# The first stage of an 8-expert layer rewritten: transposed input, rows scattered whole to their slots, expert blocks loaded by plain transfers

## The chip, the cores and the metric

The kernel runs on one core of a Trainium2 chip. The metric is the device time of one execution in microseconds. A core has the engines PE (matmul), DVE (elementwise, reductions), ACT (activations, copies), POOL (here: the indirect DMAs) and SP (plain DMAs). They run on their own and wait for each other by semaphores.

## The reference

x is 128 x 64 x 256 (8,192 tokens of 256 values). A modulated linear layer makes `hidden`; a top-2 router sends each token to 2 of 8 experts of at most CAP = 2,560 tokens; each expert is a two-layer network 256 → 1,024 → 256 with GELU; the weighted outputs are added to x.

```python
ys  = cond_1024 / sqrt(256)
d   = rsqrt((ys * ys) @ (w * w) + 1e-8)
hid = ((x * ys[:, None, :]) @ w) * d[:, None, :]        # per batch of 64 tokens
logits = hid @ wr.T                                      # 8192 x 8
vals, idx = top_k(logits, 2);  gate = softmax over the two
pos = cumsum(mask) - 1;  keep = pos < 2560               # slot of a token in its expert
h = gelu(hid[tokens of e] @ w1[e] + b1[e])
y = (h @ w2[e] + b2[e]) * gate
out = x + sum of y over a token's experts
```

## The kernel before

**Stage 1** goes over 16 groups of 512 tokens (4 tiles of 128). For each group PE transposes x (L436), DVE multiplies it by ys out of PSUM (L684, `scale_x`), PE multiplies by w (L473, four matmuls 128x512 in fp32, eight records), DVE multiplies by d (L741, `scale_hidden`). From that, with features on partitions, PE makes the logits (L485, 16 records) and transposes the rows back (L493); ACT copies the rows (L616) and stores them to `hidden` in DRAM (L619). DVE copies the logits (L803) and finds first and second expert, mask, gates (L811 to L853: a chain of small operations on 128x32, each of which waits for the one before). PE turns the mask into positions (L458 to L465, bf16), DVE turns these into addresses in a table in DRAM (`begin_list`, `slots`, `pay`), and POOL writes 128 entries of 8 bytes (token, gate) with each indirect DMA (L317): 8 a group, 128 in all. In DVE's order the end of the list of group g−1 stands behind the copy of the logits of group g. SP loads x (L275), stores it to out (L270), and reloads the buffer once that is written.

**Expert stage.** The tokens of an expert lie in blocks of 384 slots (SUBS = 3 tiles), at least LEAST (4) an expert and at most 7. The number is computed on the chip (`plan`). POOL gathers the rows of a block from `hidden` by the ids of the table (L324, three DMAs; L332 and L333 copy the ids), three blocks ahead. PE transposes them (L514), ACT and DVE split them into a high and a low part (L632, L903), and for each of 8 chunks f PE does a first product (L524 to L526, six matmuls 128x384), ACT the GELU (L645, twice), DVE the low part (L909), PE a second product (L536 to L538, nine matmuls 128x256) three chunks later. At a block's end DVE adds the bias (L934), multiplies by the gate (L940), and POOL adds the rows to out with three accumulating indirect DMAs (L357), of which L371 copied the ids. ACT copies an expert's bias once (L663). Weights (2 MB an expert) are loaded by SP and split by ACT and DVE during the two first blocks of the expert before. The last block also transposes and opens a block that does not exist.

The orders on the queues that the change touches: POOL runs scatters, then per block begin of adds, gathers, end of adds; SP runs x and out per group, then weights; PE runs in each block first product 2, transposes of the next block, first product 3, and so on.

Of the kernel before, what the change touches and what calls it, by code (L numbers as in the profile page):

```python
# [15 lines left out]
P = 128  # L25
# [7 lines left out]

TILES = 4
ROWS = TILES * P
GROUPS = T // ROWS
GB = ROWS // S
SUBS = 3
SLOTS = SUBS * P
BLOCKS = -(-CAP // SLOTS)  # L40
LEAST = 4
LAG = 3
TILES_E = BLOCKS * SUBS
COLS = E * TILES_E + SUBS
TABLE = P * COLS
# [3 lines left out]
assert ROWS == 512 and T % (4 * ROWS) == 0  # L49
# [5 lines left out]
NO_SLOT = float(1 << 22)  # L55
BIG = 3.0e38


def build(nc, x, cond, w, wr_t, w1, b1_t, w2, b2, ident, tri, expert_low, slot_base, token_ids,
          plan_consts, empty_table, out):  # L60
    hidden = nc.dram_tensor("hidden", [T + PAD, D], F32, kind="Internal").ap()
    table = nc.dram_tensor("table", [TABLE, 2], I32, kind="Internal").ap()


    x_rows = x.rearrange("b s d -> (b s) d").rearrange("(g j p) d -> g p j d", j=TILES, p=P)
    out_rows = out[0:T, :].rearrange("(g j p) d -> g p j d", j=TILES, p=P)
    hidden_rows = hidden[0:T, :].rearrange("(g j p) d -> g p j d", j=TILES, p=P)
    table_rows = table.rearrange("(p c) v -> p c v", p=P)
# [3 lines left out]
    with ExitStack() as ctx:  # L72
# [9 lines left out]
        ident_sb = sb("ident", [P, P])  # L82
# [6 lines left out]
        cond_sb = sb("cond", [P, D])  # L89
        w_sb = sb("w", [P, KC, D])  # L90
        wsq_sb = sb("wsq", [P, KC, D])
        wr_sb = sb("wr", [P, KC, E])
# [4 lines left out]
        zero_sb = sb("zero", [P, D])  # L97
        plan_sb = sb("plan_consts", [P, BLOCKS + (E + 1) * E])
        steps_e = sb("steps_e", [P, E, BLOCKS])
# [3 lines left out]
        plan_f = sb("plan_f", [P, E + 1])  # L103
        plan = sb("plan", [P, 2 * (E + 1)], I32)
# [8 lines left out]

        x_sb = [sb(f"x{u}", [P, TILES, D]) for u in range(2)]
        xs_t = sb("xs_t", [P, KC, ROWS])
        hid_t = sb("hid_t", [P, KC, ROWS])
        hid_sb = [sb(f"hid{u}", [P, TILES, D]) for u in range(2)]
        RE = [P, TILES, E]
        logits = sb("logits", RE)
# [5 lines left out]
        of_group = sb("of_group", [P, E], BF16)  # L125
# [3 lines left out]
        top = sb("top", [P, 2, TILES])  # L129
        low = sb("low", [P, 2, TILES])  # L130
        gap = sb("gap", [P, TILES])
        ratio = sb("ratio", [P, TILES])
        total = sb("total", [P, TILES])
        picked = sb("picked", [P, 2, TILES, E])
        slot_of = sb("slot_of", [P, 2, TILES], I32)
        low_bits = sb("low_bits", [P, 2, TILES], I32)
        high_bits = sb("high_bits", [P, 2, TILES], I32)
        slots = [sb(f"slots{u}", [P, 2, TILES], I32) for u in range(2)]
        pay = [sb(f"pay{u}", [P, 2, TILES, 2], I32) for u in range(2)]

# [4 lines left out]
        table_sb = sb("table", [P, COLS, 2], I32)  # L145
        table_first = sb("table_first", [P, LAG * SUBS, 2], I32)
        filled = sb("filled", [P, 1], I32)
        gather_ids = sb("gather_ids", [P, SUBS], I32)
        add_ids = sb("add_ids", [P, SUBS], I32)
        ids_ring = sb("ids_ring", [P, 4 * SUBS], I32)  # L150
        xg_first = sb("xg_first", [P, SUBS, D])
        xg_third = sb("xg_third", [P, SUBS, D])
        xg = sb("xg", [P, SUBS, D])
# [6 lines left out]
        y_sb = [sb(f"y{s}", [P, D]) for s in range(SUBS)]  # L160


        first_in = sem("first_in")
        const_in = sem("const_in")
        late_in = sem("late_in")
        table_empty = sem("table_empty")
        pad_zero = sem("pad_zero")
        set_dve = sem("set_dve")
        set_pe = sem("set_pe")
# [3 lines left out]
        x_loaded = [sem(f"x_loaded{u}") for u in range(2)]  # L173
        hid_stored = [sem(f"hid_stored{u}") for u in range(2)]
        scattered = [sem(f"scattered{u}") for u in range(2)]
        out_written = sem("out_written")
        added = sem("added")
        y_free = sem("y_free")
        t_done = sem("t_done")
# [3 lines left out]
        l_done = sem("l_done")  # L183
        back_done = sem("back_done")
        hid_copied = sem("hid_copied")
        step = sem("step")
        counted = sem("counted")
        mask_ready = sem("mask_ready")
        pos_done = sem("pos_done")
        gap_ready = sem("gap_ready")  # L190
        ratio_ready = sem("ratio_ready")
        pay_ready = sem("pay_ready")
# [3 lines left out]
        totals_done = sem("totals_done")  # L196
        plan_step = sem("plan_step")
        plan_ready = sem("plan_ready")

        first_loaded = sem("first_loaded")  # L200
        filled_ready = sem("filled_ready")
        table_loaded = sem("table_loaded")
        gather_listed = sem("gather_listed")
        add_listed = sem("add_listed")
        gathered_first = sem("gathered_first")
        gathered_third = sem("gathered_third")
        gathered = sem("gathered")
# [16 lines left out]
        h_bank = [bank[4], bank[5], bank[7]]  # L224
        out_filled = 16 * (SUBS + GROUPS)

        PEEL = 4

        FILLING = GROUPS - 3

# [767 lines left out]
```

## Time and profile before

| | |
|---|---|
| median of 3 runs | 1087.09 us (1080.96 to 1089.59) |
| profiled execution, its own time | 1081.37 us |
| its span | 1079.6 us |
| mean granted PE clock | 0.938 |
| PE busy | 978.0 us (91%) |
| DVE busy | 498.2 us (46%) |
| ACT busy | 487.9 us (45%) |
| POOL busy | 542.5 us (50%), 550 instructions |

Durations in a profile come from one execution. A line of the timeline or of a group names line, engine and operation, out<-in with the program's names, and the shape. In brackets stands the idle time before it and what ended it; "remote" and "another core or an unknown queue" mean that the profile found no instruction whose end fits the release. PEclk is the granted clock as a part of full speed.

### The profile page before, as it was taken

Reading aid. Unit: us, or ns where it says so; the run is one execution under the profiler, and the core shown is the slowest. Engines: PE = TensorE matmul, PEld = TensorE weight load, DVE = VectorE, ACT = ScalarE, POOL = GpSimd, SP = SyncE. Lnnn points to the kernel's source line nnn. Section 1 sums busy time; section 2 is a strip of 40 time slices with the busy share of each in tenths; the row PEclk is TensorE's granted clock in tenths of the full one; section 3 lists DMA queues with packets and bytes.
Section 4 is the critical chain, followed back from the end, with each engine's and each line's share of the span. In section 5 each row is a group of like instructions: output and inputs, shape, how many; then the busy total and the mean of one; then the engine's idle time right before and its main releaser. Section 6 shows DMA issues by size and latency. Waiting matters only on the chain.

```text
span 1079.6 us, 20555 instructions
## 1 busy us (share of the span) xinstructions
PE 978.0 (91%) x6550; PEld 925.8 (86%) x6551; DVE 498.2 (46%) x1395; ACT 487.9 (45%) x968; POOL 542.5 (50%) x550
## 2 busy tenths in 40 slices
PE   7588787439999999999999999999999999999994
PEld 4365555239999999999999999999999999999994
DVE  5454455254444534453455445444444453445342
ACT  3000001015556555655565555556555555565552
POOL 0545665753545454545454554545454536454542
PEclk9877778659999999999999999999999999999997
DMA  8454332321433432343224322432422242222322
GB/s 287 143 152 140 118 117 59 99 87 58 127 42 53 110 58 35 53 111 54 39 49 112 53 45 42 117 49 44 121 49 39 49 116 49 39 49 39 53 35 29
DMA packets 71071, 84.18 MB, mean 78 GB/s; under 512 B 11008, under 2 KB 64000, under 8 KB 70912
## 3 DMA queue, kind: packets, MB, share of 16 engines
q0 software_dynamic: 30880, 37.12, 20.8%
q1 hardware_dynamic: 30352, 37.86, 10.7%
q10 hardware_dynamic: 9824, 9.03, 2.6%
q8 instruction: 6, 0.10, 0.0%
q14 instruction: 9, 0.07, 0.0%
HBM read 47.80 MB, written 35.96 MB: 78 GB/s over the span
## 4 chain that ended last, share of the span: by engine, by line
PE 78%; another core or an unknown queue 7%; DVE 7%; issue 3%; DMA 2%; POOL 1%; ACT 0%; DVEq 0%; POOLq 0%; SPq 0%; ACTq 0%
PE bank L526 12%; PE bank L524 12%; PE bank L525 11%; PE bank L536 11%; PE bank L537 11%; PE bank L538 11%; PE bank L514 3%; PE bank L473 2%; PE bank L436 2%; PE bank L485 2%; DMA out_rows<-sb_y,sb_add_ids 1%; PE bank L493 1%; DVE sb_xs_t L684 1%; POOL out_rows L357 1%
## 5 line engine op out<-in xcount | busy, mean ns | idle before, releaser
L645 ACT ACTIVATE sb_h_raw<-bank,sb_b_now 128x384 f32<-128x384 f32 x370 | 216.4, 585 | 313.7 <-PE bank L526 297.1
L909 DVE TENSOR_TENSOR sb_h_lo<-sb_h_raw,sb_h_hi 128x384 fp32r<-128x384 f32 x370 | 206.1, 558 | 328.8 <-ACT sb_h_hi L645 298.9
L536 PE MATMUL bank<-sb_w_hi,sb_h_hi 128*128 128x256 f32 x1104 | 310.1, 281 | 0.8 <-DVE sb_y L934 0.8
L537 PE MATMUL bank<-sb_w_lo,sb_h_hi 128*128 128x256 f32 x1104 | 309.5, 280 | 0.0
L538 PE MATMUL bank<-sb_w_hi,sb_h_lo 128*128 128x256 f32 x1104 | 308.1, 279 | 0.0
L524 PE MATMUL bank<-sb_xt_hi,sb_w_hi 128*128 128x384 f32 x740 | 258.2, 349 | 12.4 <-DVE sb_xt_lo L903 11.7
L357 POOL DMA_INDIRECT out_rows<-sb_y,sb_add_ids x138 | 229.4, 1662 | 66.7 <-POOL sb_add_ids L371 34.9
L525 PE MATMUL bank<-sb_xt_lo,sb_w_hi 128*128 128x384 f32 x740 | 251.0, 339 | 0.8 <-issue 0.8
L526 PE MATMUL bank<-sb_xt_hi,sb_w_lo 128*128 128x384 f32 x740 | 250.5, 339 | 0.4 <-issue 0.4
L645 ACT ACTIVATE sb_h_hi<-bank,sb_b_now 128x384 fp32r<-128x384 f32 x370 | 213.1, 576 | 0.0
L536 PEld LDWEIGHTS bank<-sb_w_hi,sb_h_hi 128*128 128x128 f32 x1104 | 207.4, 188 | 1.4 <-DVE sb_y L934 1.4
L538 PEld LDWEIGHTS bank<-sb_w_hi,sb_h_lo 128*128 128x128 f32 x1104 | 207.9, 188 | 0.0
L537 PEld LDWEIGHTS bank<-sb_w_lo,sb_h_hi 128*128 128x128 f32 x1104 | 207.5, 188 | 0.0
L317 POOL DMA_INDIRECT table<-sb_pay,sb_slots x128 | 125.6, 981 | 112.8 <-DVE sb_slots L762 69.1
L324 POOL DMA_INDIRECT sb_xg<-hidden,sb_gather_ids x132 | 137.1, 1038 | 66.7 <-POOL sb_ids_ring L333 38.3
L371 POOL COPY sb_add_ids<-sb_ids_ring 128x3 int32 x46 | 15.9, 345 | 280.8 <-DVE sb_y L940 280.8
L524 PEld LDWEIGHTS bank<-sb_xt_hi,sb_w_hi 128*128 128x128 f32 x740 | 139.7, 189 | 16.5 <-issue 16.4
L525 PEld LDWEIGHTS bank<-sb_xt_lo,sb_w_hi 128*128 128x128 f32 x740 | 140.3, 190 | 0.4 <-issue 0.4
L526 PEld LDWEIGHTS bank<-sb_xt_hi,sb_w_lo 128*128 128x128 f32 x740 | 139.8, 189 | 0.5 <-issue 0.5
L616 ACT COPY sb_hid<-bank 128x512 f32<-128x512 f32 x32 | 17.2, 588 | 176.7 <-remote 146.1
L485 PE MATMUL bank<-sb_wr,sb_hid_t 128*128 128x8 f32 x256 | 43.3, 306 | 38.2 <-DVE sb_hid_t L741 38.2
L485 PEld LDWEIGHTS bank<-sb_wr,sb_hid_t 128*128 128x128 f32 x256 | 42.6, 260 | 40.6 <-DVE sb_hid_t L741 39.7
(110 smaller groups left out, 789.6 us busy)
## 6 DMA issues: line engine op xcount, KB each, us to landing
sb_w_raw<-in_w SPq DMA_DIRECT2D x18, 1024.0 KB
out_rows<-sb_x SPq DMA_DIRECT2D x16, 512.0 KB
hidden<-sb_hid ACTq DMA_DIRECT2D x16, 512.0 KB
sb_x<-in_x SPq DMA_DIRECT2D x15, 512.0 KB
out_rows<-sb_y,sb_add_ids POOLq DMA_INDIRECT x138
sb_xg<-hidden,sb_gather_ids POOLq DMA_INDIRECT x132
table<-sb_pay,sb_slots POOLq DMA_INDIRECT x128
sb_b<-in_b SPq DMA_DIRECT2D x1, 1024.0 KB, 9.0
```

What stands on the lines that cost most here:

```text
L317: pool.indirect_dma_start(table, bass.IndirectOffsetOnAxis(slots[u][:, c, j:j + 1], axis=0), pay[u][:, c, j, :], None, bounds_check=TABLE ...
L324: pool.indirect_dma_start(into[:, s, :], None, hidden, bass.IndirectOffsetOnAxis(block_ids[:, s:s + 1], axis=0),).then_inc(landed, 16)
L357: pool.indirect_dma_start(out, bass.IndirectOffsetOnAxis(add_ids[:, s:s + 1], axis=0), y_sb[s][:, :], None, compute_op=ALU.add,).then_inc( ...
L485: mm = pe.matmul(bank[6][:, j * E:(j + 1) * E], hid_t[:, k, j * P:(j + 1) * P], wr_sb[:, k, :], start=(k == 0), stop=(k == KC - 1))
L524: pe.matmul(h, w_hi[u][:, cols], xt_hi[:, rows], start=(k == 0), stop=False)
L525: pe.matmul(h, w_hi[u][:, cols], xt_lo[:, rows], start=False, stop=False)
L526: mm = pe.matmul(h, w_lo[u][:, cols], xt_hi[:, rows], start=False, stop=(k == KC - 1))
L536: pe.matmul(y, hi, w_hi[u][:, cols], start=(f == 0), stop=False)
L537: pe.matmul(y, hi, w_lo[u][:, cols], start=False, stop=False)
L538: mm = pe.matmul(y, lo, w_hi[u][:, cols], start=False, stop=(f == FC - 1))
L645: ins = act.activation(h[f % RING][:, :], h_bank[f % H_BANKS][:, 0:SLOTS], ACT.Gelu_apprx_tanh, bias=b1_now[u][:, f:f + 1])
L909: dve.tensor_tensor(h_lo[f % RING][:, :], h_raw[f % RING][:, :], h_hi[f % RING][:, :].bitcast(F32), ALU.subtract).then_inc(h_ready, 1)
```

## The change

- x is also given transposed (`x_t`, 256 x 8,192), cond too. SP loads columns of a group into a ring of four buffers; `scale_x` multiplies them in place. Transposes L436 are gone.
- Rows and logits come from one pair of matmuls for each tile of 128 tokens (`turn_back`): the moving operand is 136 columns, the identity and half of wr beside it; both halves' logits add up in the eight columns between the two blocks of 128. The result goes into one of three PSUM banks and ACT copies it (128x264) into a row of 272 floats: 128 values, 8 logits (later gates), 128 values, token id. A ring of 5 such sets in SBUF takes the place of `hid` and of `hidden` in DRAM.
- Routing works on sets of two groups (TS = 8 tiles, 8 sets): `choose` in each even group, `positions` on PE, `find_slots` and `list_set` on DVE in each odd one, from group 3 on. The gates of all eight experts are written into the row.
- POOL scatters whole rows of 1,088 bytes into `slot_rows` in DRAM, by expert and slot: 16 DMAs a set, 128 in all. It waits for the set's list and for the landing of the set two before.
- A block is then one plain load of SP (`load_block`, 384 rows, 418 KB). It waits for the transposes of the block before (`t_done`) and for DVE's copies of gates and ids (`take_meta`, `meta_done`). Blocks 0 to 3 of expert 0 are loaded as soon as the sets that fill them are placed (`need`), block 4 after all sets are placed and the unfilled slots are filled (`fill_holes`, about one transfer of 418 KB an expert).
- In a block PE's transposes of the next block move from behind first product 2 to between first product 6 and second product 3.
- POOL keeps only the adds; gathers, id copies and the table are gone. The outputs of blocks 0 to 3 have buffers of their own, since POOL adds them after the last scatter.
- out gets x by copies from DRAM to DRAM (`copy_x`), 8 in stage 1, 8 beside the early blocks.
- The last block opens no other. LEAST is 5 instead of 4.

```diff
+            def scale_x(g):
+                tile = x_in[g % X_RING]
+                dve.wait_ge(x_loaded[g % X_RING], 16 * (g // X_RING + 1))
+                for k in range(KC):
+                    cols = tile[:, k, :].rearrange("p (b s) -> p b s", s=S)
+                    dve.tensor_tensor(cols, cols, by_batch(ys_t, k, g), ALU.mult).then_inc(xs_ready, 1)
...
+            for g in range(GROUPS):
+                s = g // 2 - 1
                 scale_hidden(g)
+                if g + 2 < GROUPS:
+                    scale_x(g + 2)
+                if g % 2 == 0 and g >= 2:
+                    choose(s)
+                if g % 2 == 1 and g >= 3:
+                    found = find_slots(s)
+                    if s == SETS - 2:
+                        early_needs()
+                    list_set(s, found)
+                if 3 <= g < 3 + PIECES:
+                    split_piece(0, g - 3, g - 2)
```

PE:

```diff
+            def turn_back(g):
 
                 pe.wait_ge(hid_ready, KC * (g + 1))
                 for j in range(TILES):
+                    t = g * TILES + j
+                    tile = back_bank[t % 3]
+                    if t >= 3:
+                        pe.wait_ge(row_copied, t - 2)
+                    pe.matmul(tile[:, 0:P + E], hid_t[g % 2][:, 0, j * P:(j + 1) * P], back_sb[:, 0:P + E],
+                              start=True, stop=True)
+                    pe.matmul(tile[:, P:2 * P + E], hid_t[g % 2][:, 1, j * P:(j + 1) * P],
+                              back_sb[:, P + E:2 * (P + E)], start=False, stop=True,
+                              skip_group_check=True).then_inc(back_done, 1)
...
+            modulate(0)
+            for g in range(1, GROUPS):
+                modulate(g)
+                if g >= 3 and g % 2 == 1:
+                    positions((g - 3) // 2)
+                turn_back(g - 1)
+            turn_back(GROUPS - 1)
...
                 first_product(u, 2)
-                pe.wait_ge(gathered, b * (16 * SUBS) + 16 * SUBS)
-                transpose_block()
...
+                for f in range(3, FC):
                     bank_read(b, f - 3)
                     first_product(u, f)
+                    if f == 3:
+                        pe.wait_ge(y_read, b * SUBS + SUBS)
+                    if f - 3 == TURN and u_next is not None:
+                        pe.wait_ge(block_loaded, b * 16 + 32)
+                        transpose_block()
                     chunk_split(b, f - 3)
                     second_product(u, f - 3)
```

POOL and SP:

```diff
+            for s in range(SETS):
+                if s >= 2:
+                    pool.wait_ge(placed[s % 2], sets_placed(s - 2))
+                else:
+                    pool.wait_ge(slots_zero, 16)
+                pool.wait_ge(list_ready, s + 1)
+                for j in range(TS):
                     for c in range(TOP_K):
                         pool.indirect_dma_start(
+                            slot_rows, bass.IndirectOffsetOnAxis(slots[s % ROW_RING][:, c, j:j + 1], axis=0),
+                            rows[s % ROW_RING][:, j, :], None, bounds_check=SLOT_ROWS - 1, oob_is_err=False,
+                        ).then_inc(placed[s % 2], 16)
...
+            def load_block(e, j, b):
+                sp.wait_ge(t_done, b)
+                sp.sem_inc(sp_paced)
+                sp.wait_ge(meta_done, b)
+                sp.sem_inc(sp_paced)
+                sp.dma_start(xg[:, :, :], block_rows(e, j)).then_inc(block_loaded, 16)
```

## Rows read from the trace of the kernel before

**Rows 1.** Windows of the whole run; engines' busy time (instructions), PEclk, DMA share, GB/s.

```profile
160.00:180.00 20.00, 16.01 (x74) 10.29 (x73) 11.56 (x59) 2.56 (x6) 11.56 (x12) 0.83 0.26 79
...
400.00:640.00 240.00, 238.94 (x1709) 237.70 (x1709) 111.23 (x237) 132.82 (x262) 120.43 (x121) 1.00 0.32 61
```

**Rows 2.** Timeline; start us, us, engine, line, operation: first first-product; bias copies.

```profile
239.31 0.66 PE L524 MATMUL bank<-sb_xt_hi,sb_w_hi 128*128 128x384 f32 x1 [6.71 <-DVE sb_xt_lo L903]
...
330.95 0.22 ACT L663 COPY sb_b_now<-sb_b 128x8 f32 x1
...
954.40 0.21 ACT L663 COPY sb_b_now<-sb_b 128x8 f32 x1
```

**Rows 3.** Page, part 5: count | busy us, mean ns | idle before.

```profile
L357 POOL DMA_INDIRECT out_rows<-sb_y,sb_add_ids x138 | 229.4, 1662 | 66.7 <-POOL sb_add_ids L371 34.9
...
L317 POOL DMA_INDIRECT table<-sb_pay,sb_slots x128 | 125.6, 981 | 112.8 <-DVE sb_slots L762 69.1
L324 POOL DMA_INDIRECT sb_xg<-hidden,sb_gather_ids x132 | 137.1, 1038 | 66.7 <-POOL sb_ids_ring L333 38.3
```

**Rows 4.** Page, part 4: what the chain that ended last consists of.

```profile
PE 78%; another core or an unknown queue 7%; DVE 7%; issue 3%; DMA 2%; POOL 1%; ACT 0%; DVEq 0%; POOLq 0%; SPq 0%; ACTq 0%
```

**Rows 5.** Timeline of one group, stage 1; in brackets idle before and releaser.

```profile
162.47 0.19 DVE L836 TENSOR_TENSOR sb_first<-sb_expert_low,sb_low 128x32 f32<-128x32 f32 x1
...
163.17 0.97 POOL L317 DMA_INDIRECT table<-sb_pay,sb_slots  x1 [2.07 <-issue]
...
166.06 2.91 PE L485 MATMUL bank<-sb_wr,sb_hid_t 128*128 128x8 f32 x16 [0.49 <-DVE sb_hid_t L741]
...
172.12 0.97 POOL L317 DMA_INDIRECT table<-sb_pay,sb_slots  x1 [0.31 <-issue]
...
174.69 0.19 DVE L803 COPY sb_logits<-bank 128x32 f32<-128x32 f32 x1 [5.89 <-remote]
...
176.59 0.97 POOL L317 DMA_INDIRECT table<-sb_pay,sb_slots  x1 [3.50 <-DVE sb_slots L762]
```

**Rows 6.** Timeline of the first stream of scatters.

```profile
33.31 1.86 PE L485 MATMUL bank<-sb_wr,sb_hid_t 128*128 128x8 f32 x16
...
35.93 3.60 PE L473 MATMUL bank<-sb_xs_t,sb_w 128*128 128x512 f32 x8
...
50.02 0.97 POOL L317 DMA_INDIRECT table<-sb_pay,sb_slots  x1 [0.30 <-issue]
...
53.59 1.29 DVE L741 TENSOR_TENSOR sb_hid_t<-bank,sb_d_t 128x512 f32<-128x512 f32 x2 [12.01 <-remote]
```

**Rows 7.** Waits of 60 to 200 us: total us, times, longest.

```profile
ACT sb_hid L616 <- remote: 106.9, 10, 11.1
DVE sb_logits L803 <- remote: 52.0, 11, 6.0
```

**Rows 8.** Timeline beside six weight pieces.

```profile
234.54 3.69 DVE L720 TENSOR_TENSOR sb_w_lo<-sb_w_raw,sb_w_hi 128x512 fp32r<-128x512 f32 x6
...
236.38 1.50 POOL L317 DMA_INDIRECT table<-sb_pay,sb_slots  x1 [0.31 <-issue]
```

**Rows 9.** Chain of waits: start us, us, what.

```profile
15.93 1.21 DVE sb_hid_t L741 x2
```

**Rows 10.** DMA issues: count, KB each, us from issue to landing.

```profile
sb_b<-in_b SPq DMA_DIRECT2D x1, 1024.0 KB, 9.0
...
sb_table<-table SPq DMA_DIRECT2D x1, 171.0 KB, 2.6
```

**Rows 11.** Timeline of the end.

```profile
1065.08 0.28 PE L538 MATMUL bank<-sb_w_hi,sb_h_lo 128*128 128x256 f32 x1
...
1066.27 0.34 DVE L940 TENSOR_SCALAR sb_y<-sb_y,sb_table 128x256 f32<-128x256 f32 x1
...
1067.30 0.35 DVE L940 TENSOR_SCALAR sb_y<-sb_y,sb_table 128x256 f32<-128x256 f32 x1 [0.18 <-issue]
1067.96 1.58 POOL L357 DMA_INDIRECT out_rows<-sb_y,sb_add_ids  x1 [0.80 <-DVE sb_y L940]
```

More of the change, by code:

```diff
@@ new lines, in _ @@
+            n_holes = sp.value_load(holes[0:1, E:E + 1], min_val=E, max_val=E * LEAST)
+            sp.wait_ge(filled, n_holes * 16 + 16)
+            sp.sem_inc(sp_paced)
+            for s in range(SETS - 2, SETS):
+                sp.wait_ge(placed[s % 2], sets_placed(s))
+            sp.wait_ge(plan_ready, 1)
+            _, end = plan_of(sp, 0)
+            with sp.Fori(EARLY, end) as b:
+                load_block(0, b, b)
+            sp.wait_ge(w_lo_done, PIECES * 2)
+            load_weights(2)
@@ L424, in _ @@
-            rest = all_blocks(pool, less=1)
-            one_block(rest, E * TILES_E)
-            for i in (1, 2):
-                begin_adds(rest + i)
-                end_adds(rest + i)
+                    pool.indirect_dma_start(
+                        out, bass.IndirectOffsetOnAxis(ids[:, s:s + 1], axis=0),
+                        y[s], None, compute_op=ALU.add,
+                    ).then_inc(added, 16)
+                pool.wait_ge(added, b * (16 * SUBS) + 16 * SUBS)
+            for j in range(EARLY):
+                add_block(y_early[j], add_early[j], j)
@@ L732, in over_e, with whole, mark, after @@
                 return a.unsqueeze(2).to_broadcast(RE)
-            SPLIT_GROUPS = (0, GROUPS - 1)
+            def whole(make, *args):
+                with nc.allow_low_precision(reason="whole numbers below 2**24"):
+                    return make(*args)
+            count = [0]
+            def mark(ins):
+                count[0] += 1
+                ins.then_inc(step, 1)
+                return count[0]
+            def after(n):
+                dve.wait_ge(step, n)
             def scale_hidden(g):
+                if g >= 2:
+                    dve.wait_ge(back_done, TILES * (g - 1))
@@ new lines, in expert @@
+            def expert(u, e, start, end):
+                for j in range(2):
+                    one_block(u, e, start + j, j * len(SPLIT_AT), y_later, add_later)
+                with dve.Fori(start + 2, end) as b:
+                    one_block(u, e, b, None, y_later, add_later)
+            _, end = plan_of(dve, 0)
+            for j in range(EARLY):
+                one_block(0, 0, j, j * len(SPLIT_AT) if j < 2 else None, y_early[j], add_early[j], early=True)
+            with dve.Fori(EARLY, end) as b:
+                one_block(0, 0, b, None, y_later, add_later)
@@ L954, in constants @@
+            with dve.Fori(0, E // 2 - 1) as pair:
+                for u in (1, 0):
+                    e = pair * 2 + (2 - u)
+                    start, end = plan_of(dve, e)
+                    expert(u, e, start, end)
+            start, end = plan_of(dve, E - 1)
+            with dve.Fori(start, end - 1) as b:
+                one_block(1, E - 1, b, None, y_later, add_later)
+            one_block(1, E - 1, end - 1, None, y_later, add_later, last=True)
 def constants():
     p = np.arange(P)
-    empty = np.zeros((TABLE, 2), np.int32)
```

948 lines of the change are left out of this document (433 added, 515 removed).

## The prediction

> **What bounds the kernel now.** I read the table of windows first [rows 1]. From 400 us on PE is busy all but one microsecond in 240 at clock 1.00: the expert stage is bound by PE. Ahead of it, from 0 to the first first-product at 239.31 [rows 2], PE is busy by half to four fifths at a granted clock of 0.83 in the window shown. So the span is a first stage of 239 us that nothing fills and 46 blocks that PE fills: the adds number 138, three to a block [rows 3].
>
> The price of a block comes from the bias copies, one at the start of each expert [rows 2]. Eight of them stand in the trace; the gaps between are 96, 107, 107, 106, 90, 107 and 108 us, so experts have 5, 6, 6, 6, 5, 6, 6 blocks and the last has 6. Between the second and the last, 35 blocks take 954.40 − 330.95 = 623.45 us, 17.81 us each.
>
> The chain of waits [rows 4] then gives 7% of the span to "another core or an unknown queue". The timeline of one group [rows 5] shows what that is. The 16 router matmuls L485 end at 166.06 + 2.91 = 168.97, yet the copy of their result, L803, starts at 174.69 after 5.89 us idle; POOL issues the eight scatters of a group from 163.17 to 173.09. PE's completion is seen only once the stream of scatters is over. In a stream of 16 it is worse: PE's L473 end near 35.93 + 3.60 = 39.5, DVE's L741 that needs them starts at 53.59, 2.6 us after the stream's end at 50.99 [rows 6]. The waits of 60 to 200 us sum it: ACT 106.9 us in 10 waits and DVE 52.0 us in 11, all of them for PE results [rows 7]. So in the first stage POOL's scatters set the pace twice: 128 of them, and each burst holds the next group back. Of a group's 13.4 us (163.17 to 176.59) the burst is 9.9.
>
> **The change, part by part.** 46 blocks (LEAST 5 adds none, as every expert has at least 5) stay as they are, but for the last, which loses the next block's transposes (six records, 0.7 us) and two idle first products (2 × 1.06): −2.8 us.
>
> *PE and DVE in stage 1.* Transposes of x go; rows and logits come from 16 matmul records of 136 columns a group in place of 16 + 8 records. The records of 128x512 take 3.60 us a group at full clock [rows 6]; 16 records of 136 columns lie between L485's pace of 0.116 (1.86 for 16 [rows 6]) and that of 512 columns: I take 2.0 us, and 0.3 for the positions. So PE needs 5.9 us a group. DVE for two groups has 4 pairs of 128x512 at 1.29 [rows 6], 13 dependent routing steps like L836 (0.19 [rows 5], here on twice the elements; with the step between them I take 0.25: 3.2), the list, some ten such steps, 2.5, and two weight pieces at 3.69 / 6 [rows 8] 1.3: 12.2 us, 6.1 a group. ACT's four copies of 128x264 move what its two of 128x512 did, and are hidden. Both engines end at about 6.1 a group. The first L741 was at 15.93 [rows 9]; its successor stays near 16.5. Stage 1 for PE would end at 16.5 + 16 × 6.1 + 5 = 119, if no one holds it.
>
> *POOL.* The same count, 128 scatters, but of 1,088-byte rows instead of 8 bytes. Issue is 0.98 us and a gap of 0.30 for 8 bytes [rows 3, 6], 1.04 for a gather of 1 KB rows, 1.66 for an accumulating scatter of 1 KB rows [rows 3]. So the price of one lies between 1.28 and 1.96 us. A plain write is nearest to the gather (no read of the target): 1.04 + 0.30 = 1.34. To this comes DVE: under six L720 (both inputs in SBUF) a scatter took 1.50 in place of 0.97 [rows 8], 0.53 us for 3.69 us of such work. scale_x now has both inputs in SBUF (before, one was PSUM): 2.6 us of it for 16 scatters, 0.03 each. 1.37 × 128 = 175.4 us. The first list is ready at 16.5 + 3 × 6.1 + 2 = 36.8. Last scatter issued 212.2, landed 2.5 later (the hold's release came 2.6 after a stream [rows 6]): 214.7.
> The Trainium skill ("SBUF — State Buffer", SBUF: two separate sides) says that a DVE operation with two SBUF inputs holds a lock against GpSimd operations which read SBUF, and blocks them whole. The stretched scatter agrees in direction, at 0.53 us for six such operations and not for each; were each in-place multiply to block for its whole 0.65 us, 32 × 0.65 = 21 us would come in place of the 4 counted, and the sum would be 1008 instead of 991.
>
> *The start of the blocks.* By my count of the routing of these inputs (token sets of 1,024) expert 0's blocks 0 to 3 need 2, 4, 6 and 7 sets, so they run at 119 to 204 with small stalls: set 7 is placed at 192, block 3's load wants 184. Block 4 needs all eight. Its load: 418 KB between a load of 171 KB at 2.6 us and one of 1,024 KB at 9.0 [rows 10], by the line between them 4.4, with 0.4 to issue. So block 4's transposes start at 214.7 + 4.8 = 219.5, inside block 3, of which 9.3 us are then left (transposes 0.7, five second products, three first products). From there 42 blocks × 17.81 = 748.0.
>
> *Gathers, ids, the table* (132 gathers and 4 copies a block) leave POOL, which then has only the adds: three by 1.96, 5.9 us of 17.8. In the steady state the next block's load is issued when DVE has multiplied the old block (2.3 us after its last matmul: 1067.65 against 1065.36 [rows 11]) and copied gates and ids, in all some 3.5 us into the block; it lands 4.4 later at 7.9, and its transposes stand at 17.8 − 9.3 = 8.5: hidden by 0.6 us, and what it is later than that comes on every block. Copying x to out without passing SBUF moves the same bytes; the DMA share is 0.26 in the group's window [rows 1], no limit. One fill of 418 KB per expert lies under blocks.
>
> *Tail.* Before, 1079.6 − 1065.36 (end of the last matmul [rows 11]) = 14.2 us; the ids copy between the first multiply's end (1066.61) and the first add (1067.96) goes, 1.3 us: 12.9.
>
> *Sum.* 219.5 + 9.3 + 748.0 − 2.8 + 12.9 = 986.9 us of span. The profiled execution of before took 1081.37 for a span of 1079.6: +1.8, 988.7. Its median was 5.7 above that, its lowest 0.4 below; I add the middle, 2.5: **991 us**.
>
> Bounds of this case: 1.28 a scatter, −11.5; every in-place multiply costing the 0.53 us seen once, 32 × 0.53 − 4 = +13; landing times and the stalls before block 4, −9 to +16: 970 to 1020. At 1.96 a scatter, +75: 1066.
>
> **Rivals.**
> *The hold repeats* (the other side). Scatters now come 16 at a time, 21.9 us, and nearly without pause, while PE's ring of three row banks and every list hang on PE completions. For it: 21 such waits in 140 us [rows 7], and the longest behind the longest stream [rows 6]. Against it: in the block stage POOL is as busy (120 of 240 us [rows 1]) with gathers and adds of 1 KB rows beside a PE that hardly stops, so long rows or short streams may be spared. If it repeats whole, a set takes the stream 21.9, release 1.7, and then what waited: rest of the turn-back 2.6, choose 3.2, positions 0.6, list 2.2, a pause q of 10.3. PE then starts the blocks at 36.8 + 7 × (21.9 + q) + 3 = 193 + 7q = 265 and nothing later stops it: 46 × 17.81 + 2.1 − 2.8 = 818.6, + 12.9 + 1.8 and 2.5: 1101. In general 1029 + 7q: no gain from q = 8.3 on, slower than 1% from q = 10.
> *A partial hold*: DVE's mean wait now is 52.0 / 11 = 4.7 us [rows 7]; with q between 0 and 6 the time is 1030 to 1071, where the accumulate's price for a scatter falls too.
> *PE sets the pace* (scatters overlap better than their records show, or issue is shorter for long rows): 119 + 818.6 + 4.8 for plan and list + 12.9 + 1.8 = 957.
> *Block loads come late.* Load, gates and ids are one chain through DVE; each microsecond late costs some 45. From 2.1 us late on (a load of 7.1 us in place of 4.4) the gain of 96 us is gone. On SP an expert's last block load stands ahead of 2 MB of weights, and the next block load behind their issue; two transfers of 1,024 KB at 9.0 [rows 10] are over before it in all but the shortest wait. Against late loads: 1 MB took those 9.0 us beside other loads.
>
> **How the numbers follow.** POOL-paced, 970 to 1020: 0.44; forecast 991. PE-paced, about 957: 0.05. Partial hold or dear scatters, 1030 to 1071: 0.19. Full hold, 1075 to 1110: 0.27. Late loads, above 1050: 0.05. About 1% is what a measurement of this kernel can tell from no change, so the bounds are 1076 and 1098: faster 0.44 + 0.05 + 0.19 + 0.01 = 0.69; the hold is shared between same, 0.14, and slower, 0.17. The range for 8 in 10 leaves out the PE-paced case and the upper part of the hold: 965 to 1102; the likeliest case alone has 970 to 1020.
>
> **What would show it.** Right: first first-product near 119; scatters back to back at 1.34 to 1.40 from 37 to 212; no idle longer than 2 us before the row copies on ACT; block 4's transposes right behind the last scatter. The hold: row copies and L741's successor idle "remote" until a stream's end, gaps of 5 to 10 us between streams, first product after 200. Late loads: PE idle at each block before the transposes, released by the block load. Wrong price: scatter records above 1.3 us. The sum is wrong if the block's pace moves from 17.8, because 46 multiplies it.

## The result, and the profile after

| | before | after |
|---|---|---|
| median | 1086.26 us (4 runs, 1080.96 to 1089.59) | 1052.47 us (4 runs, 1046.39 to 1057.75) |
| ratio after / before | | 0.969, 95% interval 0.9625 to 0.9758 |
| profiled execution, span | 1079.6 us | 1049.7 us |
| first first-product | 239.31 | 208.77 |

The kernel is 3.1% faster. The forecast was 991 us, 95 less than before; 34 came. The time lies in the range given, and in the place of the rival "a partial hold" (1030 to 1071). Medians and ratios, here and below, are of fast runs: runs more than 1.5% above the fastest of the same kernel in their group are left out.

The windows of the changed kernel's run, as in [rows 1] (engines' busy time with counts in the order PE, PE's weight loads, DVE, ACT, POOL, then PEclk, DMA share, GB/s):

```profile
60.00:80.00 20.00, 6.93 (x12) 3.28 (x12) 0.31 (x1) 0.76 (x2) 15.14 (x16) 0.59 0.44 162
...
100.00:120.00 20.00, 17.52 (x94) 10.58 (x92) 16.11 (x57) 5.59 (x15) 15.66 (x14) 1.00 0.87 266
...
140.00:160.00 20.00, 0.60 (x3) 0.28 (x2) 3.71 (x13) 0.00 (x0) 14.52 (x15) 0.50 0.28 100
...
400.00:640.00 240.00, 240.00 (x1733) 239.32 (x1732) 114.26 (x276) 133.32 (x265) 63.80 (x40) 1.00 0.34 72
```

The expert stage is filled as before: PE is busy 240.00 of 240. But of the first stage, PE is busy 6.93 us in one window of 20 and 0.60 in another, while POOL is busy 15.14 and 14.52 in the same two. In the window from 100 on, with POOL just as busy, PE gets 17.52. The timeline of the worst stretch (start us, us, engine, line; in brackets the idle time before and its releaser):

```profile
142.02 0.97 POOL L363 DMA_INDIRECT slot_rows<-sb_rows,sb_slots  x1 [1.52 <-DVE sb_rows L793]
...
147.46 0.69 DVE L734 TENSOR_TENSOR sb_hid_t<-bank,sb_d_t 128x512 f32<-128x512 f32 x1 [6.30 <-remote]
...
157.91 0.69 DVE L734 TENSOR_TENSOR sb_hid_t<-bank,sb_d_t 128x512 f32<-128x512 f32 x1 [9.77 <-remote]
...
161.63 0.97 POOL L363 DMA_INDIRECT slot_rows<-sb_rows,sb_slots  x1 [0.30 <-issue]
164.91 0.38 ACT L583 COPY sb_rows<-bank 128x264 f32<-128x264 f32 x1 [25.53 <-remote]
...
165.34 0.82 PE L417 MATMUL bank<-sb_back,sb_hid_t 128*128 128x136 f32 x2 [24.74 <-ACT sb_rows L583]
...
166.40 6.00 PE L405 MATMUL bank<-sb_x,sb_w 128*128 128x512 f32 x8
...
174.44 3.60 PE L405 MATMUL bank<-sb_x,sb_w 128*128 128x512 f32 x8
...
177.84 0.97 POOL L363 DMA_INDIRECT slot_rows<-sb_rows,sb_slots  x1 [15.24 <-DVE sb_rows L793]
```

POOL issues the 16 scatters of a set without a gap from 142.02 to 162.60. In that time DVE's L734 is let through twice, after 6.30 and 9.77 us of idle, for matmuls that had ended long before; ACT's row copy L583 waits 25.53 us and starts 2.3 us after the last scatter is issued, and PE then starts at once (165.34), because its ring of row banks waited for that copy. The trace also records when a semaphore was updated: the matmuls that this copy waited for ended at 140.60, and their update is recorded at 164.88. POOL in turn stands idle for 15.24 us until the list of the next set, 177.84. This is the picture of [rows 5] and [rows 6], with longer streams.

A hold costs twice, since PE comes out of it at the lower clock: the windows above show a granted clock of 0.59 and 0.50 (the 1.2 GHz level) where PE is busy for 6.93 and 0.60 us of 20, and 1.00 (2.4 GHz) where it is busy for 17.52. The eight records of 128x512 from 166.40 take 6.00 us, those from 174.44 take 3.60.

The waits of 0 to 260 us (total us, times, longest):

```profile
ACT sb_rows L583 <- remote: 73.3, 11, 25.5
...
DVE sb_hid_t L734 <- remote: 18.3, 3, 9.8
```

The blocks start, and the stall in block 0 that is again a result seen late:

```profile
208.77 0.65 PE L472 MATMUL bank<-sb_xt_hi,sb_w_hi 128*128 128x384 f32 x1 [0.34 <-issue]
...
227.32 0.55 PE L484 MATMUL bank<-sb_w_hi,sb_h_hi 128*128 128x256 f32 x1 [4.82 <-remote]
```

The bias copies, one an expert, of which these are the first, the second and the last (as in [rows 2]):

```profile
208.40 0.18 ACT L626 COPY sb_b_now<-sb_b 128x8 f32<-128x8 f32 x1
...
319.79 0.21 ACT L626 COPY sb_b_now<-sb_b 128x8 f32 x1
...
931.48 0.21 ACT L626 COPY sb_b_now<-sb_b 128x8 f32<-128x8 f32 x1
```

From 319.79 to 931.48 are 35 blocks: 17.48 us each, against 17.81. Expert 0 has 111.39 us for its 5 blocks, 24.0 more than 5 × 17.48. The window over them shows where they went:

```profile
208.80:320.00 111.20, 94.64 (x613) 92.39 (x614) 45.24 (x125) 49.47 (x99) 48.39 (x41) 0.89 0.56 156
```

PE is idle for 16.6 us of it and busy for 94.64 where five blocks at full clock need 87.4: some 7 of the 24 us come with the granted clock of 0.89. The page's groups (count | busy us, mean ns | idle before), as in [rows 3]:

```profile
L375 POOL DMA_INDIRECT out_rows<-sb_y,sb_add_later x126 | 201.4, 1598 | 525.3 <-DVE sb_y L915 471.7
...
L472 PE MATMUL bank<-sb_xt_hi,sb_w_hi 128*128 128x384 f32 x736 | 250.8, 341 | 9.3 <-issue 3.6
...
L363 POOL DMA_INDIRECT slot_rows<-sb_rows,sb_slots x128 | 129.4, 1011 | 120.9 <-issue 79.6
```

The scatter of 1,088 bytes takes 1,011 ns a record, 30 more than the one of 8 bytes and 27 less than the gather. The end, as in [rows 11]:

```profile
1037.85 0.28 PE L486 MATMUL bank<-sb_w_hi,sb_h_lo 128*128 128x256 f32 x1
...
1039.81 1.54 POOL L375 DMA_INDIRECT out_rows<-sb_y,sb_add_later  x1 [9.13 <-DVE sb_y L915]
```

The last matmul ends at 1038.13, 11.6 us before the span's end (before: 14.2).

### The profile page after: what moved, and what is told of

Its sections match the earlier page's. It is cut to its first block, busy times and chain, and to the rows that moved or that the text cites. A ratio compares the mean times of both kernels' runs of the same rounds, so it can differ in the third digit from the quotient of the medians.

```text
span 1049.7 us, 18506 instructions
## 1 busy us (share of the span) xinstructions
PE 923.2 (88%) x6284; PEld 877.7 (84%) x6285; DVE 477.8 (46%) x1264; ACT 483.1 (46%) x978; POOL 350.7 (33%) x270
## 3 DMA queue, kind: packets, MB, share of 16 engines
q1 hardware_dynamic: 38496, 58.32, 18.5%
q0 software_dynamic: 26016, 35.93, 18.5%
## 4 chain that ended last, share of the span: by engine, by line
PE 84%; another core or an unknown queue 6%; issue 5%; DVE 2%; ACT 1%; DMA 0%; POOL 0%; POOLq 0%; DVEq 0%; ACTq 0%
PE bank L474 13%; PE bank L472 12%; PE bank L473 12%; PE bank L484 12%; PE bank L485 12%; PE bank L486 12%; PE bank L405 4%; PE bank L462 3%; PE bank L417 2%; PE bank L419 1%; ACT sb_rows L583 1%; DMA sb_ys_t<-in_cond_t 0%; POOL out_rows L375 0%; DVE sb_x L676 0%
## 5 line engine op out<-in xcount | busy, mean ns | idle before, releaser
L375 POOL DMA_INDIRECT out_rows<-sb_y,sb_add_later x126 | 201.4, 1598 | 525.3 <-DVE sb_y L915 471.7
L484 PE MATMUL bank<-sb_w_hi,sb_h_hi 128*128 128x256 f32 x1104 | 313.5, 284 | 5.9 <-remote 4.8
L472 PE MATMUL bank<-sb_xt_hi,sb_w_hi 128*128 128x384 f32 x736 | 250.8, 341 | 9.3 <-issue 3.6
L486 PEld LDWEIGHTS bank<-sb_w_hi,sb_h_lo 128*128 128x128 f32 x1104 | 211.0, 191 | 0.5 <-issue 0.5
L363 POOL DMA_INDIRECT slot_rows<-sb_rows,sb_slots x128 | 129.4, 1011 | 120.9 <-issue 79.6
L583 ACT COPY sb_rows<-bank 128x264 f32<-128x264 f32 x64 | 23.9, 379 | 163.5 <-remote 73.3
L417 PE MATMUL bank<-sb_back,sb_hid_t 128*128 128x136 f32 x128 | 30.9, 327 | 64.2 <-issue 38.3
L823 DVE TENSOR_TENSOR sb_xt_lo<-bank,sb_xt_hi 128x384 fp32r<-128x384 f32 x92 | 47.0, 552 | 78.8 <-ACT sb_xt_hi L601 73.9
L417 PEld LDWEIGHTS bank<-sb_back,sb_hid_t 128*128 128x128 f32 x128 | 22.9, 216 | 70.6 <-issue 43.6
L601 ACT CAST sb_xt_hi<-bank 128x384 fp32r<-128x384 f32 x92 | 39.6, 481 | 83.3 <-PE bank L474 77.4
```

The source lines that it names most:

```text
L363: pool.indirect_dma_start(slot_rows, bass.IndirectOffsetOnAxis(slots[s % ROW_RING][:, c, j:j + 1], axis=0), rows[s % ROW_RING][:, j, :], N ...
L375: pool.indirect_dma_start(out, bass.IndirectOffsetOnAxis(ids[:, s:s + 1], axis=0), y[s], None, compute_op=ALU.add,).then_inc(added, 16)
L417: pe.matmul(tile[:, 0:P + E], hid_t[g % 2][:, 0, j * P:(j + 1) * P], back_sb[:, 0:P + E], start=True, stop=True)
L472: pe.matmul(h, w_hi[u][:, cols], xt_hi[:, rows], start=(k == 0), stop=False)
L484: pe.matmul(y, hi, w_hi[u][:, cols], start=(f == 0), stop=False)
L486: mm = pe.matmul(y, lo, w_hi[u][:, cols], start=False, stop=(f == FC - 1))
```

## The experiments

The theory after these traces: a stream of indirect DMAs issued by POOL keeps PE's completions from being seen (**theory A**). Against it: the first stage is slow by its own chain of PE, DVE and ACT (**B**).

The kernels ran in six groups, each on one chip together with the kernel before. Before took 1021 to 1022 us in three of them (e1, e4, e5; single runs 1020.5 to 1024.2) and 1076 to 1090 in the other three (e2, e3, e6; single runs 1074.2 to 1098.8), near the 1086 of the first result. I call these groups without and with the hold. No trace of the kernel before is from a group without it, so for that kernel the hold's absence there is read from the time alone. One chip number stands on both a group with (e2) and one without (e5), so what decides it is not known. Times are compared within a group. The kernels without the sorting and e3_indirect_seq ran once each.

| kernel | group | before | this | first first-product |
|---|---|---|---|---|
| rows stored by ACT's queue (e1_plain_hw) | without | 1021.3 | 937.0 | 113.7 |
| the same (e4_plain_hw) | without | 1022.0 | 936.6 | 113.3 |
| plain DMAs of POOL (e1_plain_sw) | without | 1021.3 | 933.9 | 114* |
| the same (e2_plain_sw) | with | 1076.1 | 932.4 | 112.6 |
| changed kernel (e5_after) | without | 1022.0 | 975.0 | 119.4 |
| changed kernel (e2_after) | with | 1076.1 | 1040.7 | 199.5 |
| changed kernel (e3_after) | with | 1090.2 | 1044.3 | 199.0 |
| indirect, consecutive addresses (e3_indirect_seq) | with | 1090.2 | 1043.4 | 203* |
| landing awaited every 4 (e1_paced4) | without | 1021.3 | 1056.3 | 151* |
| the same (e3_paced4) | with | 1090.2 | 1055.5 | 149.7 |
| every 8 (e1_paced8) | without | 1021.3 | 1014.9 | 134.0 |
| the same (e3_paced8) | with | 1090.2 | 1017.1 | 132.0 |
| every 16 (e4_paced16) | without | 1022.0 | 993.9 | 125.8 |
| the same (e5_paced16) | without | 1022.0 | 994.5 | 126* |
| the same (e6_paced16) | with | 1086.2 | 1029.0 | 186.2 |
| 4 fills after every 8 (e4_work8) | without | 1022.0 | 1015.1 | 129.8 |
| before, paced (e4_before_paced4) | without | 1022.0 | 1099.7 | 260.4 |

(*: read from the first bias copy or from the first record that the trace kept.)

### Without POOL's indirect DMAs

The edit of the plain DMAs of POOL, in short; in all kernels of this part a fixed fill also takes the place of the holes, and in the form with ACT's queue two DMAs a set take the place of POOL's loop:

```diff
-                        pool.indirect_dma_start(slot_rows, IndirectOffsetOnAxis(slots[...]), rows[...][:, j, :], ...)
+                        first = s * ROWS_E + (c * TS + j) * P
+                        pool.dma_start(slot_rows[first:first + P, :], rows[s % ROW_RING][:, j, :])
```

e1_plain_hw: 

> Left out: the sorting of rows to experts. POOL scatters nothing; ACT's queue stores the 1,024 rows of set s twice, in order, into the slots of expert s (2 plain DMAs a set in place of 16 indirect ones, same bytes), and a fixed fill takes the place of the holes. Theory A (a stream of DMAs issued by POOL keeps PE's completions from being seen): no 'remote' wait of more than 2 us in stage 1, first first-product near 120 instead of 208.8, expert 0 without its 24 us of stalls, span 1049.7 - 89 - 24 = 937. Theory B (the first stage is slow by its own chain PE, DVE, ACT, whatever POOL does): first first-product at 200 or later, span 1040 or more.

e1_plain_sw: 

> Left out: the sorting of rows to experts. POOL issues the same 16 DMAs a set of 128 rows of 1,088 bytes, but plain ones to consecutive rows in place of indirect ones; a fixed fill takes the place of the holes. Theory A (any stream of DMAs whose descriptors POOL makes): remote waits of 10 us and more as in the changed kernel, first first-product within 185 to 225, span 1030 to 1065. Theory C (it is the indirect form or the scattered addresses): like the kernel with plain stores from ACT's queue, first first-product near 120 to 150, span 940 to 990.

e2_plain_sw: 

> Left out: the sorting of rows to experts (plain DMAs of POOL to consecutive rows in place of indirect ones, a fixed fill in place of the holes). On the other chip it took 934 us with no remote wait. If this chip is of the kind where before takes 1086: Theory A (any stream of DMAs of POOL holds PE) 1030 to 1065 with remote waits; Theory C (only indirect ones) 934 again. If this chip is of the kind of 1021: 934 again under both, and the indirect form itself is what costs against it.

e4_plain_hw: 

> Left out: the sorting of rows to experts (2 plain DMAs of ACT's queue a set). The price of everything but the scatters, on this chip: 935 as on the other one, with the first first-product near 114, whichever kind the chip is.

The two rows of e2_plain_sw, POOL's first 16 DMAs and the first first-product, in a group with the hold:

```profile
40.87 8.76 POOL L364 DMA_DIRECT2D slot_rows<-sb_rows  x16 [40.44 <-DVE sb_rows L792]
...
112.61 0.66 PE L471 MATMUL bank<-sb_xt_hi,sb_w_hi 128*128 128x384 f32 x1 [1.10 <-issue]
```

Theory B falls: with the same chain of PE, DVE and ACT the first stage ends at 113 us. No wait of these kernels ends on "remote". The plain form is also cheaper to issue, 8.76 us for 16, 0.55 each. That makes its streams short and puts a pause of 2 to 3 us behind each, so these runs alone don't tell the form from the length.

### The changed kernel in both kinds of group

e2_after: 

> The changed kernel again, as it is. The four runs before were made on a chip on which the kernel before takes 1021 us in place of 1086. Theory A' (PE's completions are held behind POOL's streams, and how much depends on the chip): on a chip where before takes about 1021, no remote waits, first first-product near 120, POOL's 128 scatters end by 41 + 171 = 212, block 4 and all after it follow from there: span 212 + 2 + 4.8 + 9.3 + 42 x 17.48 - 2.8 + 11.6 = 971, gain 5%; on one where it takes about 1086, 1050 again with first first-product near 209, gain 3%. Theory D (that chip is faster in everything, by 6%): after at 1050 x 0.94 = 987 with its first first-product at 196 and the same remote waits.

e2_before: 

> The kernel before again, for its trace on this chip. Theory A': where it takes about 1021 us, the waits of L616 and L803 for remote are gone and the first first-product comes near 239 - 60 = 179, while the pace of a block stays at 17.8 us. Theory D: the pace of a block is 16.8.

e5_after: 

> The changed kernel as it is. On a chip where before takes about 1022 (no hold): 975, first first-product near 120, last scatter near 212. On a chip that holds: 1044 again.

The kernel before, profiled in the group e2 (which turned out to be one with the hold; first first-product at 257.3), with its waits as in [rows 7], here of 0 to 260 us:

```profile
ACT sb_hid L616 <- remote: 146.4, 12, 19.2
...
DVE sb_logits L803 <- remote: 49.5, 11, 5.8
```

The changed kernel in e5, without the hold: first first-product, last scatter, load of block 4, its transposes; then its bias copies, and what is waited for until 300 us.

```profile
119.42 0.66 PE L472 MATMUL bank<-sb_xt_hi,sb_w_hi 128*128 128x384 f32 x1 [0.22 <-issue]
...
212.32 1.11 POOL L363 DMA_INDIRECT slot_rows<-sb_rows,sb_slots  x1 [0.31 <-issue]
...
215.91 0.42 SPq L295 DMA_DIRECT2D sb_xg<-slot_rows  x1
...
220.00 1.54 PE L462 MATMUL bank<-sb_back,sb_xg 128*128 128x128 f32 x6 [7.00 <-DMA sb_xg<-slot_rows]
```

Its second and last bias copy:

```profile
243.93 0.22 ACT L626 COPY sb_b_now<-sb_b 128x8 f32 x1
...
855.67 0.21 ACT L626 COPY sb_b_now<-sb_b 128x8 f32<-128x8 f32 x1
```

```profile
PE bank L462 <- DMA sb_xg<-slot_rows: 29.9, 4, 18.8
...
ACT sb_rows L583 <- DMA slot_rows<-sb_rows,sb_slots: 10.4, 1, 10.4
```

No wait is "remote" now, although POOL issues 113 scatters in a row from 41.47 to 191.47; PE waits for block loads, that is for POOL's scatters, as the forecast had it. Theory D (everything 6% faster) falls: the pace of a block is 17.48 in both e5_after (855.67 − 243.93 = 611.74 us for 35 blocks) and the first profile. The ratio of e5_after to before is 0.954 (0.952 to 0.955), that of e2_after 0.966 (0.952 to 0.980). Across groups, the hold costs the changed kernel 66 (e2) or 69 us (e3) over the 975.0 of e5, and the kernel before 54 to 68 us over 1022.0.

### Addresses or form

The edit in short, with `at` for the column of set, choice and tile; the fixed fill is in this kernel too:

```diff
-    slot_rows, IndirectOffsetOnAxis(slots[s % ROW_RING][:, c, j:j + 1], axis=0),
+    slot_rows, IndirectOffsetOnAxis(ids_sb[:, at:at + 1], axis=0),   # set s, consecutive rows of expert s
```

e3_indirect_seq: 

> Left out: the sorting of rows to experts. The scatters stay indirect DMAs of POOL, 128 of them with addresses read from SBUF, but the addresses are consecutive rows (set s into expert s's slots), and a fixed fill takes the place of the holes: the same destinations as the kernel with plain DMAs, and the form of the changed kernel. On a chip where before takes about 1088 us: Theory C1 (the indirect form holds PE's completions): remote waits and first first-product at 185 to 225, span 1030 to 1065. Theory C2 (scattered addresses in DRAM do it): no remote waits, first first-product near 113 to 125, span 985 or less. On a chip of 1021: no hold in either, span near 971.

e3_after: 

> The changed kernel as it is, as the measure for the others on this chip: 1038 to 1060 where before takes about 1088, about 973 where it takes 1021.

```profile
ACT sb_rows L584 <- remote: 101.0, 15, 26.1
...
DVE sb_hid_t L735 <- remote: 23.8, 5, 9.7
```

The waits of e3_indirect_seq are those of the changed kernel, and so is its time (1043.4 and 1044.3). So the hold doesn't need scattered addresses; nor does it need long rows, since the kernel before has it with 8 bytes [rows 6]. Whether the size changes its length was not tested.

### The length of a stream

```diff
                         ).then_inc(placed[s % 2], 16)
+                        n = j * TOP_K + c + 1
+                        if n % 8 == 0:
+                            pool.wait_ge(placed[s % 2], SET_ROWS * (s // 2) + 16 * n)
```

e1_paced4: 

> After every 4 scatters POOL waits until they have landed. Theory A with release at the end of a stream: no PE completion is held for more than 7 us (4 x 1.28 and 2.1 for landing), the first first-product comes before 160, POOL ends at 40.9 + 32 x 7.2 = 271, block 4 then sets the end: 271 + 4.8 + 9.3 + 42 x 17.48 - 2.8 + 11.6 = 1028 of span. Theory B: the longer POOL time comes on top, first first-product 250 or later, span 1090 or more.

e1_paced8: 

> After every 8 scatters POOL waits until they have landed. Theory A with release at the end of a stream: PE completions held up to 12 us, first first-product 150 to 190, POOL's last scatter at 40.9 + 16 x 12.3 = 238 if it never waits for a list, span 995 to 1030. Theory B: first first-product 230 or later, span 1070 or more.

e3_paced4: 

> POOL waits for the landing after every 4 scatters. On a chip that holds: if a hold ends when a stream's DMAs have landed, PE completions are late by at most 7 us, first first-product near 150, and the time is POOL's as on the other chip: 1056. If the hold has no regard to that, PE's waits come on top: 1090 or more. On a chip that doesn't: 1056.

e3_paced8: 

> POOL waits for the landing after every 8 scatters. On a chip that holds: late by at most 12 us, and the gain in PE's waits is about as large as POOL's loss (16 x 2.3 = 37 us): 1015 to 1045. If landing does not end a hold: 1080. On a chip that doesn't hold: 1015, which is 40 more than the changed kernel.

e4_paced16: 

> POOL waits for the landing once a set, after 16 scatters. It loses 8 x 2.3 = 18 us instead of the 37 of a wait after every 8. On a chip that holds: if holds grow with the stream beyond some ten DMAs, PE is late by up to 15 us in each set, first first-product 150 to 190, span 1010 to 1040. If a stream of 16 is still short enough: first first-product near 125, last scatter at 41 + 164 + 20 + 5 = 230, span 230 + 2 + 4.8 + 9.3 + 734 - 2.8 + 11.6 = 989. On a chip that doesn't hold: 989 under both.

e5_paced16: 

> A wait for the landing once a set. On a chip without the hold 994 again, which is some 19 more than the changed kernel there. On a chip that holds: a hold grows with the stream; with streams of 8 it was at most 3.2 us, so with 16 I expect up to 12 us a set and a first first-product at 150 to 190: 1010 to 1035, between paced8's 1017 and the changed kernel's 1044.

e6_paced16: 

> POOL waits for the landing once a set, on a chip that holds, if this is one (before at 1075 to 1095): a hold grows with the stream; with streams of 8 it was at most 3.2 us, with 16 I expect up to 12 us a set and a first first-product at 150 to 190: 1010 to 1035. On a chip without the hold 994 again.

The waits of e3_paced8 until 300 us, with the hold:

```profile
PE bank L465 <- DMA sb_xg<-slot_rows: 53.2, 4, 34.7
...
POOL slot_rows L363 <- DMA slot_rows<-sb_rows,sb_slots: 47.1, 15, 5.7
...
ACT sb_h_raw L615 <- remote: 9.0, 3, 3.2
```

Its first first-product and its last scatter:

```profile
132.00 0.66 PE L475 MATMUL bank<-sb_xt_hi,sb_w_hi 128*128 128x384 f32 x1 [0.22 <-issue]
...
253.83 0.97 POOL L363 DMA_INDIRECT slot_rows<-sb_rows,sb_slots  x1 [0.30 <-issue]
```

With breaks after every 8 the longest remote wait is 3.2 us and PE starts the blocks at 132, 67 us sooner than in the changed kernel. POOL pays: 47.1 us in 15 waits, which ends it at 254.8 instead of 239 (e3_after). The sum is a gain: 1017.1 against 1044.3 in the same group, or 0.935 of before (0.927 to 0.944) against 0.960 (0.948 to 0.972). The landing took 2.3 us as a rule but up to 5.7 in some waits, so the last scatter came at 254 and not at 238 as I expected of e1_paced8. Every 4 costs POOL more than it frees (1055): the expectation of e1_paced4 was 1028, but 31 waits for the landing cost 90.5 us (e3_paced4), and the last scatter came at 287 in place of 271. Every 16, with the hold:

```profile
ACT sb_rows L586 <- remote: 73.4, 23, 9.8
...
ACT sb_h_raw L615 <- remote: 19.6, 4, 10.3
```

```profile
186.15 0.66 PE L475 MATMUL bank<-sb_xt_hi,sb_w_hi 128*128 128x384 f32 x1 [0.22 <-issue]
```

Remote waits of up to 10.3 us are back, and PE starts at 186: 1029.0. So, where the landing is awaited, the waits grow with the length: no remote wait with 4, up to 3.2 us with 8, 10.3 with 16; in the changed kernel, whose streams are 16 to 48 scatters long (48 in e3_after), 25.5 to 27.5. These are idle times, which also hold the time before the matmul had ended: L616 in [rows 7] is idle for up to 11.1 us, but one such copy, at 111.86, starts 3.7 us after its matmuls' end. Without the hold the order is reversed: 975.0 for the changed kernel, 994, 1015, 1056 for 16, 8 and 4.

### A pause without a landing, and the kernel before

```diff
+                        if j % 4 == 3 and c == 1:
+                            for i in range(4):
+                                pool.memset(scratch[:, :], 0.0).then_inc(worked, 1)
+                                pool.wait_ge(worked, (s * 2 + j // 4) * 4 + i + 1)
```

e4_work8: 

> After every 8 scatters POOL fills a scratch tile four times (about 2 us) instead of waiting for the landing. On a chip that holds: if it is the pause in POOL's issue that lets PE's completions through, as with the wait: 1010 to 1030, first first-product 125 to 145. If the transfers must have landed or POOL must wait on them: as the changed kernel plus the pauses, 1044 to 1080, first first-product 200 or later.

e4_before_paced4: 

> The kernel before, with POOL waiting for the landing after every 4 of the 8 scatters of a group in its loop (groups 0 to 13). On a chip that holds: Theory A says the wait of 2.2 us twice a group costs POOL less than the hold costs PE: DVE's and ACT's remote waits gone, span 1025 to 1060 against 1088. If the hold is no more than the time that POOL needs anyway: 14 x 4.4 = 62 us come on top, 1150. On a chip that doesn't hold: 1021 plus up to 62.

Both fell into a group without the hold. e4_work8 therefore says only what the pauses cost there (1015.1, as with the landing), and whether a pause alone would let PE's completions through stays open. The kernel before speaks against it: its bursts of 8 stand mostly 2.0 to 3.7 us apart, without a wait for the landing, and L803 still waited up to 6.0 us [rows 7], against 3.2 with the landing awaited; but it is another kernel. e4_before_paced4 cost 78 us where I had at most 62: the lost time seems to come on the path of every group, with more than the wait itself; I did not follow that further. What pacing would do to it with the hold was not seen.

## Why the prediction missed

**Step by step, without the hold (e5_after), the sum is right.** First first-product: 119 forecast, 119.42 measured. Scatters: 1.37 us each forecast, (212.32 − 41.47) / 127 = 1.345 measured; the first at 36.8 forecast and 41.47 measured (its list was ready at 40.42; the routing after the third group took longer than the 2 us I gave it). Last scatter: 212.2 and 212.32. Transposes of block 4: 219.5 and 220.00. From there the blocks were 0.33 us cheaper than forecast (42 of them, 14 us) and the tail 1.3 shorter, and the time is 975.0 instead of 991.

**The failed step is the choice between the rivals.** The hold was seen, named, priced at 193 + 7q for the first first-product, and given 0.27, the partial hold 0.19, against 0.44 for none. So the sum of 991 has it at 0, and it came: the first first-product stood at 208.77 where the sum had 119, and the time was 1052.5 where the same kernel without the hold takes 975.0. The reason given against it was the block stage, where POOL is as busy beside a PE that never stops. That compared busy time. The runs show that in a group with the hold the length of an unbroken stream counts: the block stage has at most five DMAs in a row, and with a landing awaited after 4 or 8 the waits are small in stage 1 too. The rows to go by were [rows 5] and [rows 6], where 8 in a row held for 5.9 us and 16 for 12; the change makes all of them 16 or more. A third place in the trace of the kernel before says the same and is not in the prediction, which reads PE as busy by half to four fifths ahead of the blocks: sixteen scatters with one gap of 0.64 us, then nine gathers, run from 188.56 to 220.76, and PE is busy 0.58 us of 20 beside them.

```profile
200.00:220.00 20.00, 0.58 (x7) 0.19 (x5) 0.89 (x3) 1.28 (x3) 14.97 (x18) 0.61 0.42 125
...
208.00 1.07 ACT L616 COPY sb_hid<-bank 128x512 f32<-128x512 f32 x2 [17.93 <-remote]
...
216.42 0.69 DVE L741 TENSOR_TENSOR sb_hid_t<-bank,sb_d_t 128x512 f32<-128x512 f32 x1 [16.18 <-remote]
```

In the profile after, PE starts at 208.8, which is q = 2.3 by the formula, but that is no measure of the pauses: these were 15.4 us ahead of set 2, 1.5 ahead of set 4, 15.2 ahead of set 5, 6.1 and 3.0 ahead of the last two, 5.9 on average. The formula put PE's start 3 us behind the first scatter of set 7; it came 18.5 us ahead of it (227.31), so that part was wrong, and that the time came near 1029 + 7q with a small q is luck.

**The forecast gain counted the hold once.** 1087 to 991 compares a kernel with the hold to one without. Pairs of like with like give half or less: 1022.0 to 975.0 is 47 us; with the hold it is 34 (first result), 35 (e2) and 46 (e3). From 1086.3 with the hold to 975.0 without are 111 us: the 47 of the change and the 64 of the hold. The forecast gain of 95 was that sum less 16, mostly for a block priced too high. The change does not remove the hold; it issues as many indirect DMAs as before in the same stage.

**Terms of the sum that were mis-sized.**
- *After the first first-product*: in the formula for the hold I let nothing stop PE after the start. Expert 0 lost 24.0 us: 16.6 of idle PE (4.82 of "remote" before 227.32, and others), while two streams still run beside blocks 0 and 1, and some 7 with the lower clock.
- *The block*: 17.48 us instead of 17.81, some 15 us over 46 blocks. Over the same 35 blocks, PE of the kernel before stands idle in 8 places, 4.9 us together (0.14 a block; five of 0.9 us are for DVE's L903), where the kernel after has no gap, and its records of 384 columns start 0.179 us apart on average against 0.175 (48 a block: 0.2). I had costed the move of the transposes and the end of the gathers at nothing for PE; which of them gave this was not taken apart.
- *Scatter price*: 1,011 ns against the 1,038 of the gather that I took; the accumulate's price, by which the time would have been 1,066 us, never showed.
- *DVE's in-place multiply* does stretch single scatters (1.40 and 1.43 us in place of 0.97), and the mean is 1.011, 0.03 above that of the 8-byte scatters. The lock rule of the Trainium skill ("SBUF — State Buffer", SBUF: two separate sides), taken as the prediction takes it, would have each of the 32 multiplies block POOL for its whole 0.65 us, 21 us in all; the mean here bounds all such loss to 128 × (1.011 − 0.97) = 5 us.
- *Late block loads* did not come: PE is busy 240.00 of 240.
- *Tail*: 11.6 instead of 12.9.

## To carry to other kernels

When a chain of waits has a share that belongs to no known engine, find out what the waits have in common before costing anything in that stretch, and ask of a change whether it makes that thing longer. Long unbroken streams of indirect DMAs can delay other engines' semaphores; short pauses in the stream may cost less than the stalls (here the changed kernel with a landing wait after every 8 scatters takes 1017 where before takes 1090 and the changed one 1044), but they are a loss of 40 us where nothing is held. A price that is compared between two kernels must be taken under the same conditions in both.

## What the runs showed of the hardware that I had not expected

- PE's completions, and in one stretch DVE's, are seen late by other engines behind a stream of indirect DMAs of POOL: waits up to 3.2 us in streams of 8 with the landing awaited (6.0 for L803 in the kernel before), 10.3 in streams of 16, 25.5 to 27.5 in the changed kernel with 16 to 48. It is there with rows of 8 and of 1,088 bytes, with scattered and with consecutive addresses. In a group without the hold, 113 in a row held nothing (e5_after).
- The same program on the same kind of chip shows this in some groups of runs and not in others: the kernel before takes 1021 to 1022 us or 1076 to 1090, and kernels without long streams of indirect DMAs take about the same in both (932.4 with, 933.9 without; paced by 8, 1017.1 and 1014.9). What decides it is open; so is the mechanism.
- The records of semaphore updates tell the two kinds of group apart even where the time does not. Without the hold nearly every update is recorded (in e5_after, 65 on the semaphore of the 64 copies L583, the last of them at the program's end); with it many are missing (48 in the trace after, 43 in e6_paced16, and 61 in e3_paced4, which takes as long as e1_paced4 with its 65). e2_plain_sw has all 65. So whatever delays the updates may also lose their records; whether the recording itself takes part in the hold is not shown.
- A plain DMA of POOL with 128 rows of 1,088 bytes is issued in 0.55 us, an indirect one in 0.97 with a gap of 0.30.
